# Second experts: the last, short chunk of the down products as high rows above low rows

## The reference

```python
B, S, H, I, E = (4, 256, 256, 704, 8)      # x itself is 8 x 256 x 256: T = 2048 tokens
router_logits = xf @ w_gate.T
routing_weights = softmax_integer(router_logits)
top_w, top_i = jax.lax.top_k(routing_weights, _TOP_K)      # _TOP_K = 2
top_w = top_w / top_w.sum(axis=-1, keepdims=True)
combine = jnp.zeros((T, E), xf.dtype).at[jnp.arange(T)[:, None], top_i].add(top_w)
for e in range(E):
    h = jax.nn.silu(xf @ w1[e].T) * (xf @ w3[e].T)         # T x 704
    out = out + combine[:, e:e + 1] * (h @ w2[e].T)        # 704 -> 256
```

## Time and profile before

| | |
|---|---|
| runs | 865.8, 867.36 and 1688.11 us, median 867.36 |
| the profiled execution | 865.74 us, its span 864.0 |
| TensorE busy | 739.3 us (86%), 4774 products |
| VectorE, ScalarE, GpSimd busy | 462.8, 260.3, 293.5 us |
| granted clock of TensorE, mean | 0.914 |
| second experts | from 530 to 855 us |

### The profile page before, as it was taken

One profiled execution on the slowest core, in us unless ns is written; L12 is line 12 of the kernel. 1 busy time (PEld: TensorE's weight loads), 2 busy tenths in 40 slices (PEclk: granted clock), 3 DMA queues, 4 the chain that ended last, 5 costly groups with the idle time before them and its releaser, 6 DMA issues.

```text
span 864.0 us, 15043 instructions
## 1 busy us (share of the span) xinstructions
PE 739.3 (86%) x4774; PEld 641.1 (74%) x4774; DVE 462.8 (54%) x1206; ACT 260.3 (30%) x523; POOL 293.5 (34%) x281
## 2 busy tenths in 40 slices
PE   4878859999999999697999625999999999899994
PEld 4656748878888888586777624888888888888884
DVE  5937666667677676704998473333333333333331
ACT  1472223222322323255676101222222222222220
POOL 3306843334343343352210043232332323323321
PEclk9885569999999999998999756999999999999997
DMA  9600126767567666596001650112424442442211
GB/s 216 266 0 2 49 95 210 244 211 240 199 218 241 206 226 212 171 430 263 14 27 37 221 211 25 26 26 37 141 41 125 136 133 37 139 130 38 31 26 18
DMA packets 55863, 114.86 MB, mean 133 GB/s; under 512 B 11680, under 2 KB 24992, under 8 KB 53376
## 3 DMA queue, kind: packets, MB, share of 16 engines
q1 hardware_dynamic: 48320, 103.87, 34.8%
q0 software_dynamic: 7488, 10.23, 7.1%
HBM read 68.86 MB, written 45.22 MB: 132 GB/s over the span
## 4 chain that ended last, share of the span: by engine, by line
PE 68%; DVE 10%; DMA 9%; issue 6%; SPq 2%; ACT 2%; POOL 1%; POOLq 0%; DVEq 0%; ACTq 0%
PE ps L912 17%; PE ps L913 15%; PE ps L914 15%; DMA down_low<-w_lo_rows 6%; PE ps L1147 2%; DMA wexp<-in_dn 2%; PE ps L1024 2%; PE ps L1033 2%; PE ps L983 2%; PE ps L813 2%; PE ps L1070 1%; PE ps L883 1%; PE ps L951 1%; PE ps L892 1%; DVE h_high L1385 1%
## 5 line engine op out<-in xcount | busy, mean ns | idle before, releaser
L518 POOL TENSOR_TENSOR part_lo<-wexp,part_hi 128x512 fp32r<-128x512 f32 x68 | 89.4, 1325 | 135.4 <-ACT part_hi L694 133.2
L593 POOL DMA_INDIRECT out_rows<-vbd,slot_row x39 | 61.8, 1586 | 212.2 <-DVE vbd L1583 172.7
L912 PE MATMUL ps<-w_hi,x_high 128*128 x312 | 105.7, 339 | 28.2 <-issue 22.6
L1604 DVE TENSOR_TENSOR arena<-arena,ps 128x704 f32<-128x704 f32 x39 | 34.6, 887 | 158.8 <-ACT arena L785 158.8
L913 PE MATMUL ps<-up_low,x_high 128*128 x312 | 101.7, 326 | 0.0
L914 PE MATMUL ps<-w_hi,x_low 128*128 x312 | 101.4, 325 | 0.0
L912 PE MATMUL ps<-xn_high,gu_high 128*128 (+3 forms) x208 | 92.7, 446 | 0.1
L912 PEld LDWEIGHTS ps<-w_hi,x_high 128*128 128x128 f32 x312 | 59.4, 190 | 38.6 <-issue 38.6
L913 PE MATMUL ps<-xn_low,gu_high 128*128 (+3 forms) x208 | 82.7, 397 | 0.0
L914 PE MATMUL ps<-xn_high,gu_low 128*128 (+3 forms) x208 | 82.6, 397 | 0.0
L683 ACT ACTIVATE wexp<-ps 128x512 f32<-128x512 f32 (+1 forms) x52 | 31.1, 599 | 160.4 <-PE ps L914 160.4
(11 more groups left out here) (271 smaller groups left out, 1654.8 us busy)
## 6 DMA issues: line engine op xcount, KB each, us to landing
wexp<-in_wexp SPq DMA_DIRECT2D x68, 256.0 KB, 3.2
w_hi_rows<-part_hi SPq DMA_DIRECT2D x68, 256.0 KB, 2.5
w_lo_rows<-part_lo SPq DMA_DIRECT2D x68, 256.0 KB, 2.0
w_hi<-w_hi_rows SPq DMA_DIRECT2D x8, 2176.0 KB, 21.5
up_low<-w_lo_rows SPq DMA_DIRECT2D x8, 1408.0 KB, 6.0
down_low<-w_lo_rows SPq DMA_DIRECT2D x8, 768.0 KB, 8.4
wexp<-in_gu SPq DMA_DIRECT2D x2, 1632.0 KB, 8.7
xn_rows<-arena SPq DMA_DIRECT2D x8, 256.0 KB, 2.1
```

The lines of the kernel that those rows point to most:

```text
L518: pool.tensor_tensor(part_lo[:, n % 2, :], part_w[:, n % 4, :], part_hi[:, n % 2, :].bitcast(F32), ALU.subtract).then_inc(p_lo, 1)
L593: pool.indirect_dma_start(out=out_rows, out_offset=bass.IndirectOffsetOnAxis(ap=slot_row[:, i:i + 1], axis=0), in_=yb[:, i % 2, :], in_off ...
L912: pe.matmul(out, high, rows_high, start=start, stop=False, skip_group_check=True)
L1604: dve.tensor_tensor(h1.rearrange("p (a n) -> p a n", a=2), sg1.rearrange("p (a n) -> p a n", a=2), bank(2, 2).rearrange("p (a n) -> p a n" ...
```

## The change

`h1` gets 64 columns more. VectorE writes its last 64 columns a second time behind themselves with a second instruction; `d_hidden` moves from the first to the second. The sixth transpose has 128 columns, so both copies lie one above the other in PSUM. ScalarE copies chunks 4 and 5 with one instruction of 128 rows. VectorE's last subtraction works on the rows 64 to 127 and writes the low part into `hT_high` itself, so the stationary tile of chunk 5 holds 64 high rows above the same 64 rows' low parts. `w_hi` of chunk 5 is loaded twice, to the rows 0 to 63 and 64 to 127. One product with it then gives high x high and low x high; a second one with `down_low`, whose rows 64 to 127 are zeros, gives high x low. `hT_low` shrinks to 5 chunks. SyncE's loads are cut: each expert's 4096 first columns as before, and the last 256 columns in two extra transfers of 64 rows (7 experts in one, 1 KB runs), then the same for expert 7.

```diff
+        TAIL = I1 - (C1 - 1) * P
...
-        h1 = view(arena, 1728, I1)
+        h1 = view(arena, 1728, I1 + TAIL)
         hT_high = view(hT_high_mem, 0, C1, P)
-        hT_low = view(hT_low_mem, 0, C1, P)
+        hT_low = view(hT_low_mem, 0, C1 - 1, P)
...
             for e in range(7):
-                sp.dma_start(w_hi[:, e * WE:(e + 1) * WE].bitcast(F32), w_hi_rows[:, e * WE:(e + 1) * WE]).then_inc(in_exp0, 16)
+                whole = slice(e * WE, (e + 1) * WE - D)
+                sp.dma_start(w_hi[:, whole].bitcast(F32), w_hi_rows[:, whole]).then_inc(in_exp0, 16)
+
+            def tail_of(rows, first, n):
+                return rows[0:TAIL, first * WE:(first + n) * WE].rearrange("p (e c) -> p e c", e=n)[:, :, WE - D:WE]
+
+            def load_tails(first, n, landed):
+                for half in range(2):
+                    to = w_hi[half * TAIL:(half + 1) * TAIL, first * WE:(first + n) * WE].bitcast(F32)
+                    sp.dma_start(to.rearrange("p (e c) -> p e c", e=n)[:, :, WE - D:WE],
+                                 tail_of(w_hi_rows, first, n)).then_inc(landed, 16)
+            load_tails(0, 7, in_exp0)
...
-            sp.dma_start(w_hi[:, last:last + WE].bitcast(F32), w_hi_rows[:, last:last + WE]).then_inc(in_exp7, 16)
+            sp.dma_start(w_hi[:, last:last + WE - D].bitcast(F32), w_hi_rows[:, last:last + WE - D]).then_inc(in_exp7, 16)
+            load_tails(7, 1, in_exp7)
...
-                act.activation(hT_high[:, 4, :], bank(5)[:, 0:P], ACT.Copy)
-                act.activation(hT_high[0:64, 5, :], bank(5)[0:64, P:2 * P], ACT.Copy).then_inc(d_hT, 1)
+                act.activation(hT_high[:, 4:6, :], bank(5)[:, 0:2 * P].rearrange("p (c n) -> p c n", n=P),
+                               ACT.Copy).then_inc(d_hT, 1)
...
                 for c in range(C1):
-                    n = min(P, I1 - c * P)
-                    mm = pe.transpose(bank(4, 2)[0:n, c * P:(c + 1) * P], h1[:, c * P:c * P + n], ident[:, :])
+                    mm = pe.transpose(bank(4, 2)[:, c * P:(c + 1) * P], h1[:, c * P:(c + 1) * P], ident[:, :])
...
-                for c in range(C1):
-                    n = min(P, I1 - c * P)
-                    mm = in_parts(bank(6)[:, 0:D], hT_high[0:n, c, :], hT_low[0:n, c, :],
-                                  w_hi[0:n, bass.ds(expert + (U1 + c * D), D)],
-                                  down_low[0:n, bass.ds(low * D1 + c * D, D)], c == 0, c == C1 - 1)
-                mm.then_inc(d_down, 1)
-
-            pe.wait_ge(in_exp0, 16 * 7)
-            pe.wait_ge(in_exp7, 16)
+                for c in range(C1 - 1):
+                    in_parts(bank(6)[:, 0:D], hT_high[:, c, :], hT_low[:, c, :],
+                             w_hi[:, bass.ds(expert + (U1 + c * D), D)],
+                             down_low[:, bass.ds(low * D1 + c * D, D)], c == 0, False)
+                c = C1 - 1
+                pe.matmul(bank(6)[:, 0:D], hT_high[:, c, :], w_hi[:, bass.ds(expert + (U1 + c * D), D)],
+                          start=False, stop=False, skip_group_check=True)
+                pe.matmul(bank(6)[:, 0:D], hT_high[:, c, :], down_low[:, bass.ds(low * D1 + c * D, D)],
+                          start=False, stop=True, skip_group_check=True).then_inc(d_down, 1)
+
+            pe.wait_ge(in_exp0, 16 * 9)
+            pe.wait_ge(in_exp7, 16 * 3)
...
-                dve.tensor_tensor(hT_low[0:64, 5, :], bank(5)[0:64, P:2 * P], hT_high[0:64, 5, :].bitcast(F32),
+                dve.tensor_tensor(hT_high[TAIL:P, 5, :], bank(5)[TAIL:P, P:2 * P], hT_high[TAIL:P, 5, :].bitcast(F32),
                                   ALU.subtract).then_inc(d_hTlow, 1)
...
-                dve.tensor_tensor(h1.rearrange("p (a n) -> p a n", a=2),
+                dve.tensor_tensor(h1[:, 0:I1].rearrange("p (a n) -> p a n", a=2),
                                   sg1.rearrange("p (a n) -> p a n", a=2),
-                                  bank(2, 2).rearrange("p (a n) -> p a n", a=2)[:, :, 0:HALF1],
+                                  bank(2, 2).rearrange("p (a n) -> p a n", a=2)[:, :, 0:HALF1], ALU.mult)
+                dve.tensor_tensor(h1[:, I1:I1 + TAIL], sg1[:, I1 - TAIL:I1], bank(3)[:, HALF1 - TAIL:HALF1],
                                   ALU.mult).then_inc(d_hidden, 1)
```

## The result

The changed kernel takes 869.6 us in the median of 20 runs (866.3 to 873.1), the kernel before 865.9 in the median of 20. The ratio is 1.0038, with a 95% interval of 1.0021 to 1.0055: slower by 3.3 us, 1.8 to 4.8. The forecast was +4.2 on the profiled execution's own time, and a time of 870.5 with 866 to 877 as its range. One of the three runs shown of before took 1688.11 us, but not one of the 17 that followed.

The account below looks back on a forecast made before the run. The prediction took silu, VectorE's product, register loads and up products to bound each block, not the array. 865.74 + 4.9 (added product) - 0.7 (end) = 869.9; it forecast 870.5 us, between bases 869.9 and 871.6, range 866 to 877.

Parts of the forecast that it names:

- What bounds the block: Second experts' blocks: silu, VectorE's product, register loads and up products set 8.16 us; the array has 0.66 us of slack.
- One down product fewer is worth 0.40 us on the array and nothing on the time: TensorE, each block: the array is done 0.40 us earlier, all of it falling into the slack.
- The added product costs 0.13: VectorE, each block: d_hidden comes 0.13 us later, +4.9 us over 38 periods (bounds +2.5 and +10.3).
- The other edits at nothing: Last transpose, ScalarE's joined copy, VectorE's moved last subtraction: hidden, costing nothing; without cover some 0.1 us a block.
- The loads: SyncE's split weight loads: land later but before they are wanted, costing nothing; without cover 3 + 1 us.
- The end: Last block: transposes start 0.4 us earlier, down products shorten, the last subtraction loses a tenth; -0.7 us taken.
- The sum: Whole kernel: 865.74 + 4.9 - 0.7 = 869.9 us, 871.6 on the higher base; forecast 870.5.
- The array: Rival, second experts' blocks: the next block follows the transposes, so 15 us and 0.7 go: 850; 3%.
- the queue: Rival, TensorE's queue: register loads start when it has room, one product earlier, saving 4.6 and 0.7 us: 860.4; 5%.
- the hidden addition: Rival, VectorE: the new instruction costs nothing, only the end counts: 865, or 867 on the higher base; 8%.
- the addition at its full length: Rival, VectorE: 0.22 to 0.27 us a block, 873.4 to 875.3, on the higher base 877; 15%.
- The clock: Rival, TensorE: its granted clock falls as its busy share drops, 2 us more per slow block, slower by over 2%; 2%.

Follow-up runs that it names:

- e1: The changed kernel without VectorE's second product, the last 64 columns of h1 being zeros: 864.25 us, ratio 0.9982 to the kernel before.
- e2: The kernel before with only VectorE's second product of 64 columns added, the signal on it and its result unused: 872.05 us, ratio 1.0067.
- e4: The kernel before with the next block's three register loads moved ahead of the wait for d_hidden on TensorE's queue: 830.5 us, ratio 0.9583.
- e5: The changed kernel with the next block's register loads moved ahead of the transposes, as in e4: 816.3 us, ratio 0.9435.
- e9: e5 with GpSimd's gather of rows for block i + 4 issued before the add of block i's result: 812.6 us, ratio 0.9387.
- e11: The kernel before without the down products of chunk 4, 3 of 18 per block left out: 865.1 us, ratio 0.9987.
- e3: The kernel before without the down products of chunks 3 and 4, 6 of 18 per block left out: 882.4 us, ratio 1.0176.
- e7: e4 with the last chunk's three products on 128 rows, zeros in the lower 64, without VectorE's second product: 818.8 us, ratio 0.9460.

## Why the prediction was right, step by step

*What bounds the block.* Right. The control with block 0 and the load at 725.7 stood for the claim; e1, e2 and e4 show it by taking the instruction away, adding it alone, and taking the register loads off the loop. One size in it was wrong: the array's slack, 0.66 us by the prediction, is 0.95 (e4). Nothing in the sum hung on it.

*One down product fewer is worth 0.40 us on the array and nothing on the time.* Right on both: 8.150 us a period in e1, and 0.42 less per period from e4 to e5 once the array binds. My split was 0.12 for the product and 0.28 for the edges; it is 0.09 and 0.33.

*The added product costs 0.13.* Measured 0.120 a period in the change and 0.133 alone; its duration is 214 ns where the fit gave 0.22, its overlap 0.08 where I took 0.09. The prediction set one sentence of the Trainium skill (VectorE: DVE Perf Modes, The DRAIN you can't avoid) against such an overlap, and read too little of it: the same section says that a next op that is not held starts earlier. L1622 starts 0.08 us before L1619 ends, as L1588 did before the end of L1604, so the trace agrees with the section as a whole.

*The other edits at nothing.* Right as a group: e1 holds them all and is not slower than before. The last subtraction is a small surprise inside. L1612 starts at 708.02, just when L1611 ends (707.73 + 0.28), where before L1597 began at 728.79 and L1596, at 728.59 + 0.28, ended 0.08 later. The Trainium skill, VectorE: DVE Perf Modes, Two Vector instructions with no wait between them, says that an instruction whose operands start in another group of 32 partitions than the last one's is held until all before it have finished; by that rule the 64 lower rows cost the overlap, and the trace agrees. It is off the path except in the last block.

*The loads.* At the cost I gave, none. The low parts are asked for at 500.06 in place of 498.45, 1.6 us later as block 0 is, and block 1 starts at 542.13; e1 has these loads too and is not slower than before.

*The end.* Here a term was mis-sized: I took -0.7 us and it came to nothing. From the last block's start to the end of its weighting input the profiles show 9.14 + 3.61 = 12.75 before and 8.93 + 3.84 = 12.77 after. The first part did get shorter, by 0.21 where I had reckoned 0.3 (0.4 for the transposes less 0.1 for the last subtraction). But the 17 down products took longer than the 18 had: the granted clock was 0.56 over them, against 0.66 over those of before.

```profile
842.25:851.39 9.14, 7.25 (x49) 6.72 (x49) 3.52 (x8) 2.08 (x7) 2.77 (x2) 1.00 0.14 14
851.39:855.00 3.61, 3.57 (x18) 3.05 (x18) 0.00 (x1) 0.00 (x0) 0.00 (x0) 0.66 0.32 36
```

That is one execution of each, and where the clock falls at the end differs from execution to execution. In the profiles of e1 (17 products) and e2 (18, three of them on 64 rows) it did not fall there; their last down products alone:

```profile
852.61:854.90 2.29, 2.29 (x17) 2.08 (x17) 0.00 (x0) 0.00 (x0) 0.00 (x0) 1.00 0.48 57
858.38:860.98 2.60, 2.60 (x18) 2.26 (x18) 0.00 (x0) 0.00 (x0) 0.00 (x0) 1.00 0.46 50
```

With these in place of the slow ones the end would be 8.93 + 2.29 against 9.14 + 2.60, an estimated 0.5 us shorter. By this estimate the saving is there, nearly in the size forecast, and what the clock does in the same few microseconds can hide it: the prediction took the clock there as the same in both kernels.

*The sum.* In the two profiled executions the spans differ by 6.1 us: 37 x 0.120 = 4.4 for the periods, nothing at the end, and 1.7 because block 1 starts at 542.13 in place of 540.47. That last part is there when block 0 starts (531.93 in place of 530.17), and it is not the change: e5 and e9, which contain the change, start block 0 at 529.65 and 531.13, and over all kernels of the study it starts between 529.65 and 535.0. Against 20 runs of each kernel the difference is 3.3 us, and the 4.4 of the periods is inside its interval. The forecast of +4.2 lies this close to 4.4 partly by luck: 0.13 in place of 0.120 a period made it 0.5 too long, and the end 0.7 too short.

*The rivals.* The array and the queue are refuted by e1 and e11, the hidden addition by e2, and the addition at its full length by 0.120 and 0.133 a period where it would be 0.22 to 0.27. The clock did not fall in the changed kernel (1.00 over all 37 periods). But I had given this rival 2% on the strength of one window, and e3 shows that it is real in this very stage: less work for an array that does not bind cost 16 us, some 1.5 for each of the 11 blocks where I had reckoned 2. The changed kernel had 41 products per block left of 42, e11 39 and e3 36; only the last fell.

## What to carry to other kernels

A busy engine is not a bound. Ask what the last instruction before each idle gap in its queue waited for: here 0.66 us of "issue" in 8.16, under an array busy for 92% of the time, were register loads queued behind a semaphore, and moving them gained 4.2% where taking work off the array gained nothing. Find that out before judging an edit to the array: the same change lost 3.3 us in front of this loop and won 14 behind it.

When an edit shortens one engine's work at the price of a small instruction on another, price the small one on its own path: 0.21 us of duration, less the overlap with its neighbour, times the number of blocks.

## What the runs showed of the hardware that I had not expected

Products on 64 rows next to products on 128 rows cost 0.33 us for three at the full clock, about as much as three more full-height products; padding them with zero rows (e7) took that back. And TensorE's granted clock can fall in a stage that looks evenly busy: in e3, where the array never idled for more than 1.44 us at a time, it fell to about half for a part of eleven of the 37 periods; in the kernel before, in the changed one and in e11 it stayed at 1.00 over all 37. What makes the difference stays open.
